# Two graph layers on one core: GpSimd clears a small scratch tile behind each of its row transfers

## What is computed

```python
# layer 0: gated messages, summed by destination, then an update of every node
edge_input = concat([x[src], edge_attr_32])
messages   = gelu(edge_input @ mW1 + mb1) @ mW2 + mb2
gates      = sigmoid(gelu(edge_input @ gW1 + gb1) @ gW2 + gb2)
aggregated = segment_sum(messages * gates, dst)
update     = gelu(concat([x, aggregated]) @ uW1 + ub1) @ uW2 + ub2
x1         = layernorm(x + (layernorm(x + update) * ln_g + ln_b))
# layer 1: attention over the edges of each destination, 8 heads of 12
score = exp(clip(sum_head(K(x1)[src] * Q(x1)[dst] * E(edge_attr_96)) / sqrt(12), -5, 5))
h     = segment_sum(V(x1)[src] * score, dst) / (segment_sum(score, dst) + 1e-6)
out   = layernorm(x1 + h)
```

## Time and profile before

| | us |
|---|---|
| median of 3 runs | 1965.96 |
| lowest and highest | 1957.66, 1973.78 |
| span of the profiled execution | 1985.4 |
| GpSimd busy in it | 936.1 |
| TensorE matmul busy | 1110.7 |
| VectorE busy | 944.9 |
| ScalarE busy | 688.5 |

### The profile page before, as it was taken

One profiled execution on the slowest core, in us unless ns is written; L12 is line 12 of the kernel. 1 busy time (PEld: TensorE's weight loads), 2 busy tenths in 40 slices (PEclk: granted clock), 3 DMA queues, 4 the chain that ended last, 5 costly groups with the idle time before them and its releaser, 6 DMA issues. The chain is left out here.

```text
span 1985.4 us, 26381 instructions
## 1 busy us (share of the span) xinstructions
PE 1110.7 (56%) x5213; PEld 683.8 (34%) x5213; DVE 944.9 (48%) x4243; ACT 688.5 (35%) x1523; POOL 936.1 (47%) x978
## 2 busy tenths in 40 slices
PE   2211159993111389888989783120577752167784
PEld 1100025551000158776777672010233321023331
DVE  1000014441000038988789788000577761168886
ACT  0000015451000125776677567100343430034443
POOL 7777700006777340434333433777243357544444
PEclk9555559996555579999899886555888885589896
DMA  4222216662111033656455453222233331123341
GB/s 112 64 58 59 55 57 185 187 189 82 48 48 49 28 104 125 188 182 195 138 191 180 155 179 123 78 59 59 66 103 101 101 81 47 48 66 117 103 111 38
DMA packets 179806, 206.38 MB, mean 104 GB/s; under 512 B 110572, under 2 KB 124846, under 8 KB 179739
## 3 DMA queue, kind: packets, MB, share of 16 engines
q1 hardware_dynamic: 140709, 159.21, 25.8%
q0 software_dynamic: 31168, 45.88, 9.5%
q10 hardware_dynamic: 7862, 0.67, 0.3%
HBM read 101.29 MB, written 77.64 MB: 90 GB/s over the span
## 5 line engine op out<-in xcount | busy, mean ns | idle before, releaser
L460 POOL DMA_INDIRECT rows<-agg_d,dst_at x194 | 184.4, 951 | 335.7 <-DMA agg_d<-node_work 246.8
L441 POOL DMA_INDIRECT agg_d<-rows,put_at x196 | 188.3, 961 | 291.4 <-issue 253.9
L482 POOL DMA_INDIRECT out<-rows,put_at x196 | 190.8, 974 | 173.2 <-ACT rows L762 107.5
L475 POOL DMA_INDIRECT node_work<-agg_d,src_i x193 | 182.5, 946 | 183.7 <-DMA x_in<-node_work 126.8
L871 DVE SCALAR_TENSOR_TENSOR ps<-hidden,ps 96x512 f32<-96x512 f32 x49 | 33.9, 692 | 418.1 <-ACT hidden L706 309.6
L544 PE MATMUL ps<-hidden,mW2s 97*96 97x512 f32 x98 | 63.0, 729 | 293.9 <-issue 216.6
L432 POOL DMA_INDIRECT rows<-in_x,src_i x195 | 189.8, 973 | 63.2 <-issue 60.4
L624 PE MATMUL ps<-nT,Wks 96*96 96x512 f32 x98 | 68.1, 784 | 231.3 <-issue 126.3
L727 ACT ACTIVATE node_work<-node_work,nshift,nscale 128x96 f32<-128x96 f32 x392 | 145.5, 454 | 80.4 <-DVE nshift L995 70.6
L772 ACT ACTIVATE nT<-ps 96x512 f32<-96x512 f32 x99 | 56.3, 589 | 252.2 <-remote 167.3
L493 PE MATMUL ps<-ident,x_in 128*96 128x128 f32 x588 | 83.1, 278 | 86.7 <-DMA ea<-in_edge_attr 64.8
(11 more groups left out here) (152 smaller groups left out, 2471.1 us busy)
## 6 DMA issues: line engine op xcount, KB each, us to landing
agg_d<-zeros SPq DMA_DIRECT2D x40, 480.0 KB
x_in<-in_x SPq DMA_DIRECT2D x49, 384.0 KB
node_work<-agg_d SPq DMA_DIRECT2D x49, 384.0 KB
agg_d<-node_work SPq DMA_DIRECT2D x49, 384.0 KB
out<-node_work SPq DMA_DIRECT2D x49, 384.0 KB
mask<-cont_d SPq DMA_DIRECT2D x49, 208.0 KB
ein<-rows SPq DMA_DIRECT2D x49, 192.0 KB
mask<-cont_d SPq DMA_DIRECT2D x49, 192.0 KB
```

The lines of the kernel that those rows point to most:

```text
L441: pool.indirect_dma_start(agg_d, rows_at(put_at, g, j), rows[:, g * EJ + j, :], None).then_inc(agg_added[g % 2][j], 16)
L460: pool.indirect_dma_start(rows[:, g * EJ + j, :], None, x1_d, rows_at(dst_at, g, j)).then_inc(xd_gathered[g % 3][j], 16)
L475: pool.indirect_dma_start(ahead[:, g % AHEAD, j, :], None, x1_d, rows_at(src_i, g, j)).then_inc(x1s_gathered[g % 2][j], 16)
L482: pool.indirect_dma_start(out, rows_at(put_at, g, j), rows[:, g * EJ + j, :], None, bounds_check=N - 1, oob_is_err=False).then_inc(out_sca ...
```

## The change

Behind each of the 974 row transfers GpSimd's program clears a scratch tile `pause` of 128 partitions by 64 floats, which nobody reads. Each clear counts on the semaphore `rested`, and the next clear first waits for the one before it. `breathe()` is called in all five passes, directly behind the transfer; the first pass stands here for the others. The clear of `tail_rows` now counts on `pads_set` as its ninth, and SyncE waits for nine where it waited for `tail_set`.

```diff
+PAUSE = 64
...
+        pause = sb("pause", [P, PAUSE])
...
+        rested = sem("rested")
-        tail_loaded, tail_set, tail_gathered = sem("tail_loaded"), sem("tail_set"), sem("tail_gathered")
+        tail_loaded, tail_gathered = sem("tail_loaded"), sem("tail_gathered")
...
-            sp.wait_ge(tail_set, 1)
+            sp.wait_ge(pads_set, 9)
...
+            pauses = itertools.count(1)
+
+            def breathe():
+
+                n = next(pauses)
+                if n > 1:
+                    pool.wait_ge(rested, n - 1)
+                pool.memset(pause[:, :], 0.0).then_inc(rested, 1)
+
...
                     pool.indirect_dma_start(rows[:, g * EJ + j, :], None, x, rows_at(src_i, g, j)).then_inc(xs_gathered[g % 2][j], 16)
+                    breathe()
...
-            dve.memset(tail_rows[:, :, :], 0.0).then_inc(tail_set, 1)
+            dve.memset(tail_rows[:, :, :], 0.0).then_inc(pads_set, 1)
```

More of the change, by code:

```diff
@@ L19 @@
+import itertools
 from contextlib import ExitStack
```

## The result

The changed kernel takes 1936.49 us (median of 4 runs, 1932.28 to 1937.17) beside 1963.52 us of the kernel before on the same chip (4 runs): a ratio of 0.990, 95% interval 0.986 to 0.994. That is faster by 1%, where 1535 us was forecast. The profiled execution has a span of 1935.4 us, 50 less than that of before, whose profile lay 1% above its median; the medians are 27 us apart.

What follows compares the result with a forecast made beforehand. GpSimd's dense transfers, every 1.25 us, were taken to overload something shared, so GpSimd and the other engines work in turns. At 1.50 us the five passes would overlap the steps, ending at 1550 us profiled, 1535 as median; range 1307 to 1810.

Steps and rivals of the forecast that it cites:

- crawl: Beside GpSimd's back-to-back transfers all sequencers slow down: SyncE's assertion takes 700 ns instead of 31.
- Step 1, the clear: Clear behind each of 974 transfers: 0.16 us, raising the period from 1.25 to 1.50 us, bounds 1.30 to 1.71.
- The skill's estimate: GpSimd clear at 1.03 to 1.8 cycles an element: 0.05 to 0.10 us for 64, period 1.30 to 1.35, below 1.40.
- Step 2, the wait: Wait for the clear before: nothing in calm; with sequencers slowed, clear and wait cost 0.70 us each, period at least 1.40.
- the reading of pass five: Fifth pass has one register move more a transfer, 699 ns when slowed; at 1.75 us a transfer the backlog shrinks.
- The service time of 1.40: Something behind GpSimd, shared by all sequencers, digests one transfer in 1.40 us; feeding every 1.25 us builds a backlog.
- The terms of the sum beyond the limit: Period over 1.40, no backlog: first pass to 296 us, edge steps 8 us, update steps 11, attention steps 14 and 12.
- The lower end of the range: All low bounds, period 1.41, nothing stretched: edges end at 290, updates at 819, 49 attention steps of 9.6; 1320, median 1307.
- Step 4: Clear of the tail rows counts on another semaphore and SyncE waits for 9 in place of 1: costs nothing.
- Hidden clear: Rival: the clear falls into the transfer's 0.30 us of issue, period stays 1.25, time stays 1966 us; chance 0.07.
- Partial relief: Rival: backlog goes, but sharing at 93% is nearly as bad, 20 us an edge step, 1850 us; chance 0.08.
- The rival that the clear only adds: Slowed sequencers stay and each dense transfer pays: 2055 us at 0.16 us each, 2220 at 0.46; chance 0.11.

Runs made afterwards that it cites:

- the ring at 1.49: Against the kernel before: clears of 320 columns on four scratch tiles in turn, each waiting for the clear four transfers before; 1738.7 us, 0.876, on a chip with slowed sequencers.
- the rings of 256 to 320 columns: Against the kernel before: clears of 256, 288, 320 columns on four scratch tiles in turn, each waiting for the clear four transfers before; ratios 0.945, 0.916, 0.876.

## Why the prediction was wrong, by its steps

- *What bounds the kernel.* Right for the chip of the profile. The turns go with the rate of transfers: the same program at 1.55 us a transfer has none. That some chips have no crawl at all could not be seen in a profile of one.
- *Step 1, the clear.* Its duration was right, 166 ns for 0.16 us. What failed is "I take 1.50, since a clear stands between instructions of another kind and some issue is likely". The clear lies in the 0.30 us of issue that stood there before, and the period is 1.28, outside of the bounds of 1.30 to 1.71, which I had built on the lower side by hiding all but the columns. The hidden part was 0.14 us. This is the step on which the sum fell, for it stood under the condition that the period exceeds 1.40. It is close to the sign that the prediction had set down for it, "period under 1.40 with the assertion at 700 ns": 1.28, and assertions of 3 to 700 ns with a median of 356.
- *The skill's estimate.* The Trainium skill's GPSIMD Engine Reference, Performance versus the Vector engine, led to 1.30 to 1.35 with the crawl still entered. The trace's 1.28 and the crawl agree with that far better than my 1.50. Its low end of 1.03 cycles an element, 0.86 ns at 1.2 GHz as an estimate, is also near the 0.83 ns a column of the wider clears.
- *Step 2, the wait.* "So even with a period of 1.30 to 1.40 a backlog would be entered and left again" failed. Clear and wait were priced from the register move of pass five, 0.70 us each. The wait alone does nothing to the crawl (ratio 0.997, 4 scans in 253 us), so the reading of pass five, that one extra instruction a transfer limits the crawl by itself, does not hold in general. The clear does hold GpSimd itself back, to 1.43 on average and not 2.1, and that buys the 1%; but 1.43 lies inside the crawl. "I take nothing in the calm state" also failed: where nothing crawls the wait lays open the register loads of the third pass, 44 us.
- *The service time of 1.40, and "a backlog never forms" above it.* As the pace at which GpSimd itself gets along once it is held up, 1.40 was nearly right: 1.43 to 1.44 in both kernels. As the limit above which the others run free it was mis-sized. A period of 1.44 still crawls, 1.49 half, 1.55 hardly. With my period of 1.50 the forecast of 1535 would have been some 200 us short: the ring at 1.49 took 1739.
- *The terms of the sum beyond the limit.* Near at 1.55, and in part by luck. First pass to 306 us (forecast 296), edge steps 6.2 us ((306 - 27)/45, the first scan at 27 us; forecast 8, bound 6), end at 1523 (forecast 1550). The second pass followed the first at once, as forecast. But the path behind it was another: the update and attention steps were priced too high, and the third to fifth pass are not held up by them but are GpSimd's own, 194 x 1.55 = 301 us. That the end is so near comes of a longer period than was forecast meeting steps that were priced too high.
- *The lower end of the range* is summed too low by its own terms. At a period of 1.41 the 974 transfers alone are 1373 us, more than the 1320 of the sum, in which GpSimd's own time is no bound; and 819, 49 steps of 9.6 and the tail of 20 are 1309.
- *Step 4* needs no price: the kernel with the wait alone has this edit too, and its ratios are 0.9995 and 0.997.
- *The rivals.* Hidden clear, the chance of 0.07, is what happened to the period, and its 1966 was the nearest figure to the result. What it missed is that a clear holds its own engine back inside the crawl. Partial relief, the chance of 0.08 (20 us an edge step and 1850 us), is what the rings of 256 to 320 columns show, with 22, 17 and 10 us between scans and 1867, 1819 and 1739 us. The rival that the clear only adds was made for a chip with the crawl and is wrong there; on chips without it the clears do only add (1.062), by other terms than its 0.16 us a transfer. The Trainium skill's sentence that "PE and ACT never wait on anyone" (SBUF — State Buffer, Who interferes with whom) stands there as a rule on SBUF ports. The chips without the crawl agree with it, where TensorE is busy for 227 of 247 us beside the transfers; taken for every kind of waiting it does not hold on the others, 52 of 253 us.

Not tried and open: what the shared thing is and what it counts (transfers, rows or their bytes); whether a pause of another kind than a clear does the same; which property or condition of a chip brings the crawl (it showed on at least two chips, on one of them at two times, and not on three others); why a 0.17 us clear makes GpSimd yield in it where a wait does not; and whether the DMAs that SyncE issues in each edge step load it too, which would explain the fading between 1.44 and 1.55 us.

## What to carry to other kernels

Before an instruction is priced on top of a repeated one, look at the idle time that the repeated one leaves: a clear of 0.17 us behind a transfer with 0.30 us of issue cost 0.03, and the period stayed where the crawl is for that. When rows show a whole core in turns with one engine's dense transfers, vary the rate in wide steps until they end (384 columns: 0.77 of the time), and do it on more than one chip, for such slowing costs 6 to 35% where nothing is congested (64 to 512 columns). If an engine needs a scratch write as a pause, let it wait for one some steps back, since a wait for the newest keeps its sequencer from running ahead over register loads.

## What the runs showed of the hardware

- The same program takes 1238 to 1239 us on some chips and 1964 to 1983 us on others. On the latter, row transfers of 128 x 96 floats every 1.25 us make a 31 ns assertion of another engine's sequencer take 700; at 1.55 us its median is 31 again (longest 537), and at 1.66 none takes over 37.
- In that state GpSimd itself is held up in the first pass, from 206 us on without clears and from 25 us on with one of 0.17 us behind each transfer; from there it gets along at 1.43 to 1.44 us a transfer on average in both.
- A clear of GpSimd over 128 partitions takes 166, 329, 383, 436, 542 and 969 ns for 64, 256, 320, 384, 512 and 1024 floats, and up to about 0.14 us of it hides in the issue time behind an indirect transfer.
- A GpSimd wait for its own newest instruction costs nothing in even stretches (0.16 us of issue with either), and 3 to 5 us where register loads stand behind it.
